# Moving the projection of the second layer's keys from the weighing pass of the first attention into its key pass

## The reference, cut to what matters

```
# layer 0: 8 heads of 64; context normed, keys rotated by position
kv_x = layer_norm(ctx) @ Wkv;  k = rope_rotate_k(k_x);  sim = q k^T;  out = softmax(sim) v
# layer 1: 16 heads of 16; context as it is
k = ctx @ wk + bk;  v = ctx @ wv + bv;  out = softmax(q k^T / 4 + mask) v
```

## Time and profile before

| | us |
|---|---|
| median of 3 runs | 2969.78 (2967.99 to 2975.21) |
| the profiled execution, its time | 2967.38 |
| its span, first to last instruction | 2965.6 |
| key pass, from its first matmul to the first transfer of the weighing pass | about 143.8 to 432.5 |
| weighing pass, to the first transfer behind it | about 432.5 to 945.5 |
| mean granted TensorE clock, share of 2.4 GHz | 0.898 |

### The profile page before, as it was taken

The page is one execution under the profiler, slowest core; times in us unless marked ns, Lnnn a source line. Parts: engine busy times, 40 slices in busy tenths (PEclk is TensorE's granted clock), DMA queues, the critical chain, the costliest instruction groups (busy, mean ns, idle before and its releaser), DMA issues. The chain is left out here.

```text
span 2965.6 us, 58913 instructions
## 1 busy us (share of the span) xinstructions
PE 2399.3 (81%) x22114; PEld 1483.9 (50%) x22114; DVE 1865.8 (63%) x3029; ACT 1212.3 (41%) x1871; POOL 479.5 (16%) x260
## 2 busy tenths in 40 slices
PE   3488869999997393999995779999995336999978
PEld 3333325555554381666663635555554323555547
DVE  7577766666766615666653248778884838777721
ACT  2145533333332324777773223233330133555542
POOL 0055530000000000000000005666551200000000
PEclk7599989999998795999997799999997567999989
DMA  7455553555541164766660523222221144676626
GB/s 238 165 179 193 194 178 101 145 145 151 153 137 57 53 227 123 164 157 158 168 135 24 191 92 115 87 87 87 87 105 34 38 105 96 150 164 149 155 59 228
DMA packets 240402, 390.69 MB, mean 132 GB/s; under 512 B 31281, under 2 KB 201622, under 8 KB 240122
## 3 DMA queue, kind: packets, MB, share of 16 engines
q1 hardware_dynamic: 240250, 388.47, 45.6%
HBM read 310.41 MB, written 78.01 MB: 131 GB/s over the span
## 5 line engine op out<-in xcount | busy, mean ns | idle before, releaser
L2271 PE MATMUL l2x_kf<-l2x_w,l2x_nin 128*128 128x512 f32 x784 | 341.6, 596 | 6.8 <-DMA l2x_nin<-scratch_nT 6.7
L1465 DVE CUSTOM_DVE_ANT_0 l1x_junk<-l1x_pm,l1x_mrow,l1x_top 128x896 bf16<-128x896 f32 x224 | 247.1, 1148 | 107.5 <-PE l1x_pm L1604 105.0
L1465 DVE CUSTOM_DVE_ANT_0 l3x_junk<-l3x_pm,l3x_mrow,l3x_top 128x896 bf16<-128x896 f32 x224 | 246.1, 1148 | 87.1 <-PE l3x_pm L1604 86.6
L1533 ACT ACTIVATE l1x_prob<-l1x_ring,l1x_mask_col 128x512 f32<-128x512 f32 x392 | 247.8, 684 | 114.0 <-PE l1x_ring L1624 112.9
L1536 ACT ACTIVATE l3x_prob<-l3x_ring 128x512 f32<-128x512 f32 x392 | 213.0, 595 | 160.5 <-PE l3x_ring L1628 160.4
L1251 POOL TENSOR_TENSOR l2x_side_rest<-l2x_side_xin,l2x_side_kp 128x1792 f32<-128x1792 f32 x14 | 50.3, 3593 | 1341.4 <-ACT l2x_side_kp L1227 1341.4
L2271 PEld LDWEIGHTS l2x_kf<-l2x_w,l2x_nin 128*128 128x128 f32 x784 | 148.5, 191 | 191.5 <-issue 189.0
L2253 ACT ACTIVATE l2x_fsq<-l2x_f 128x1024 f32<-128x1024 f32 x98 | 103.6, 1057 | 287.4 <-DVE l2x_f L2218 287.4
L2317 POOL TENSOR_TENSOR l2x_gk<-l2x_f,l2x_ks 128x1024 f32<-128x1024 f32 x98 | 182.3, 1896 | 159.9 <-DVEq L2243 159.9
L1055 PE MATMUL l0x_att_pv<-l0x_wv,l0x_att_vin 128*128 128x512 f32 x392 | 194.5, 618 | 1.3 <-DVE l0x_att_tops L936 1.3
L948 DVE TENSOR_TENSOR l0x_att_pt<-l0x_att_ps,l0x_att_tops 128x1024 f32<-128x1024 f32 x99 | 120.9, 1221 | 97.3 <-PE l0x_att_ps L1072 97.2
(11 more groups left out here) (689 smaller groups left out, 4718.8 us busy)
## 6 DMA issues: line engine op xcount, KB each, us to landing
l1x_kt<-scratch_KS SPq DMA_DIRECT2D x84, 448.0 KB, 9.1
l3x_kt<-scratch_KS SPq DMA_DIRECT2D x84, 448.0 KB, 9.1
scratch_KT<-l0x_max_kf SPq DMA_DIRECT2D x28, 896.0 KB, 3.9
l0x_att_kt<-scratch_KT SPq DMA_DIRECT2D x56, 448.0 KB, 7.5
scratch_KS<-l0x_side_kp SPq DMA_DIRECT2D x14, 1344.0 KB, 13.7
scratch_KS<-l2x_side_kp SPq DMA_DIRECT2D x14, 1344.0 KB, 6.0
l0f_w<-L_ffn_exp_w SPq DMA_DIRECT2D x16, 1024.0 KB, 7.0
l1f_w<-L_ffn_W SPq DMA_DIRECT2D x16, 1024.0 KB, 6.5
```

The costliest lines, as they stand in the source:

```text
L1465: dve.tensor_tensor_reduce(junk[x % 2][:, :, :], pm[x % 2][:, :, 0:SPLIT], mrow[b][:, :].rearrange("p (s k) -> p s k", s=2), 1.0, top[1 - ...
L1533: ins = act.activation(into, scores, ACT.Exp, bias=R.mask_col[:, bass.ds(m * TILES + n // 4, 1)])
L2271: last = pe.matmul(pf[u][:, n, :], nin[b][:, c, t * P:(t + 1) * P], w[:, c, n * BANK:(n + 1) * BANK], start=(c == 0), stop=(c == DC - 1))
```

## The change

Four edits go together.

1. **The projection moves.** The key pass also loads the raw context of its chunk (`raw`, one more transfer), PE makes two more projections for it (`other_keys`, tile `p1`, printed as `l0x_max_p`), ACT adds the bias into `k1` (printed as `l0x_max_k`), and SP spills `k1` to a new float32 tensor `scratch_K1`. In the weighing pass `side.project` and `side.evacuate` are gone; `side_xin` is loaded from `scratch_K1` instead of the raw context and split as before.
2. **PSUM.** `pb` had two banks and now has one; `p1` gets the other.
3. **The order.** ACT's order in the key pass becomes that of PE (copy, other keys, rounding, for each half), and the fold of the second half is done one step later, ahead of everything else on DVE. The signal with which PE lets SP load the next chunk (`projected`) moves behind the last `other_keys`.
4. **Two buffers for the parts.** In layer 0 `side_kp` gets two buffers, so that the high part of a chunk waits for the spill two chunks before. Layer 2's side work keeps one.

```diff
@@ rotated_keys, SP
+                    sp.dma_start(raw[b][:, :, :], raw_src[n].squeeze(0)).then_inc(sem(f"raw{b}"), 16)
...
                     sp.dma_start(kt_dram[n].squeeze(0), kf[b][:, :, :]).then_inc(sem(f"spilled{b}"), 16)
+                    after(sp, sem("k1_read"), DC * (number(b, i) + 1))
+                    sp.sem_inc(S.sem("max_begun"), 1)
+                    sp.dma_start(k1_dram[n].squeeze(0), k1[b][:, :, :]).then_inc(sem(f"k1_spilled{b}"), 16)
@@ rotated_keys, DVE
                 def both(ahead, now):
+                    fold_second_of_before(*now)
                     rotate(*ahead, 0)
-                    fold(*now, 0)
+                    fold_first(*now)
                     rotate(*ahead, 1)
-                    fold(*now, 1)
@@ rotated_keys, ACT
+                def other_keys(b, i, c):
+                    if c == 0:
+                        after(act, sem(f"k1_spilled{b}"), i * 16)
+                    after(act, sem("k1_proj"), DC * number(b, i) + c + 1)
+                    act.activation(k1[b][:, c, :], p1[:, 0:MAX_CHUNK], ACT.Identity,
+                                   bias=bias1[:, c:c + 1]).then_inc(sem("k1_read"), 1)
...
                 def both(ahead, now):
                     copy_scores(*now, 0)
+                    other_keys(*ahead, 0)
+                    round_keys(*ahead, 0)
                     copy_scores(*now, 1)
-                    round_keys(*ahead, 0)
+                    other_keys(*ahead, 1)
                     round_keys(*ahead, 1)
@@ rotated_keys, PE
-                    after(pe, sem("b_read"), 2 * number(b, i) if p == 0 else n - 1)
-                    project(pb[p], w_k, b, slice((2 + p) * P, (3 + p) * P), xin).then_inc(sem("b_proj"), 1)
+                    after(pe, sem("b_read"), n)
+                    project(pb, w_k, b, slice((2 + p) * P, (3 + p) * P), xin).then_inc(sem("b_proj"), 1)
...
+                def other_keys(b, i, c):
+                    if c == 0:
+                        after(pe, sem(f"raw{b}"), (i + 1) * 16)
+                    after(pe, sem("k1_read"), DC * number(b, i) + c)
+                    project(p1, w1, b, slice(c * P, (c + 1) * P), raw).then_inc(sem("k1_proj"), 1)
+                    if c == DC - 1:
+                        after(pe, sem("k1_proj"), DC * number(b, i) + DC)
+                        after(pe, sem("a_proj"), 2 * number(b, i) + 2)
                         pe.sem_inc(sem(f"projected{b}"), 1)
...
                 def both(ahead, now):
                     block_of_keys(*ahead, 0)
                     scores(*now, 0)
+                    other_keys(*ahead, 0)
                     block_of_keys(*ahead, 1)
                     scores(*now, 1)
+                    other_keys(*ahead, 1)
@@ attend, PE
-                        if t % TILES < 4:
-                            side.project(pe, 2 * i + t // TILES, t % TILES)
@@ SplitKeys
+        self.kp = [sb(f"kp{b}", [P, 3, DC, CHUNK], BF16) for b in range(self.per_chunk)]
```

More of the change, by code:

```diff
@@ L495, in _, with rotated_keys @@
                 start_counts(pool, S)
-def rotated_keys(nc, S, A, R, qb, w_k, bias_k, top, chunks, seed):
+def rotated_keys(nc, S, A, R, qb, w_k, bias_k, other, top, chunks, seed):
     nc = S.nc
@@ L517, in rotated_keys @@
         xin = [sb(f"xin{b}", [P, DC, MAX_CHUNK]) for b in range(2)]
+        raw = [sb(f"raw{b}", [P, DC, MAX_CHUNK]) for b in range(2)]
         cs = [sb(f"cs{b}", [P, 2, MAX_CHUNK]) for b in range(2)]
@@ L520, in rotated_keys @@
         kf = [sb(f"kf{b}", [P, 4, MAX_CHUNK]) for b in range(2)]
+        k1 = [sb(f"k1{b}", [P, DC, MAX_CHUNK]) for b in range(2)]
         kb = [sb(f"kb{b}", [P, 4, MAX_CHUNK], BF16) for b in range(2)]
@@ L524, in rotated_keys @@
         pa = [ps(f"pa{p}") for p in range(2)]
-        pb = [ps(f"pb{p}") for p in range(2)]
+        pb, p1 = ps("pb"), ps("p1")
         psc = ps("ps", HEADS)
@@ L575, in _ @@
                 dve.wait_ge(S.sem("max_started"), 3)
+                dve.memset(near[1][:, :, :], -3.0e38).then_inc(S.sem("near_begun"), 1)
+                dve.wait_ge(S.sem("near_begun"), 1)
                 for p in range(2):
@@ L914, in _ @@
                         chunks.load(sp, b, i + 1)
-                        side.spill(sp, 2 * i + b)
+                        side.spill(sp, i, b)
                 for b in range(2):
@@ L1188, in load, with spill @@
     def load(self, sp, m):
[L1189 to L1192 removed]
+        after(sp, self.sem("rest"), self.per_chunk * m)
         sp.sem_inc(self.S.sem("side_begun"), 1)
         sp.dma_start(self.xin[:, :, :], self.src[bass.ds(m, 1)].squeeze(0)).then_inc(self.sem("xin"), 16)
[L1196 removed]
+    def spill(self, sp, i, b):
+        m = 2 * i + b
         after(sp, self.sem("low"), self.per_chunk * (m + 1))
@@ L1198, in spill @@
         sp.sem_inc(self.S.sem("side_begun"), 1)
-        sp.dma_start(self.dst[bass.ds(m, 1)].squeeze(0), self.kp[:, :, :, :].rearrange(
-            "p s c k -> p (s c) k")).then_inc(self.sem("spilled"), 16)
-    def project(self, pe, m, n):
-        c, side = n // 2, n % 2
-        if n == 0:
-            after(pe, self.sem("xin"), (m + 1) * 16)
-        after(pe, self.sem("read"), 4 * m + n)
-        for d in range(DC):
-            last = pe.matmul(self.px[:, 0:SPLIT], self.w[:, d, c * P:(c + 1) * P],
-                             self.xin[:, d, side * SPLIT:(side + 1) * SPLIT], start=(d == 0), stop=(d == DC - 1))
-        last.then_inc(self.sem("projected"), 1)
@@ L1212, in evacuate @@
-    def evacuate(self, act, m, n):
-        c, side = n // 2, n % 2
-        if n == 0:
-            after(act, self.sem("rest"), 2 * m)
-        after(act, self.sem("projected"), 4 * m + n + 1)
-        act.activation(self.kf[:, c, side * SPLIT:(side + 1) * SPLIT], self.px[:, 0:SPLIT], ACT.Identity,
-                       bias=self.bias[:, c:c + 1]).then_inc(self.sem("read"), 1)
-    def high(self, act, m, c):
+        sp.dma_start(self.dst[bass.ds(m, 1)].squeeze(0), self.parts(b).rearrange(
+            "p s c k -> p (s c) k")).then_inc(self.sem(f"spilled{b}"), 16)
@@ L1221, in high, with parts @@
+    def parts(self, b):
+        return self.kp[b % len(self.kp)]
+    def high(self, act, i, b, c):
+        m = 2 * i + b
         if c == 0:
-            after(act, self.sem("spilled"), m * 16)
-        if self.proj:
-            after(act, self.sem("read"), 4 * m + 2 * c + 2)
-        elif c == 0:
+            if len(self.kp) == 2:
+                after(act, self.sem(f"spilled{b}"), i * 16)
+            else:
+                after(act, self.sem(f"spilled{1 - b}"), (i + b) * 16)
             after(act, self.sem("xin"), (m + 1) * 16)
-        act.activation(self.kp[:, 0, c, :], self.kf[:, c, :], ACT.Copy).then_inc(self.sem("high"), 1)
@@ L1255, in subtract, with finish @@
             self.sem("low"), 1)
-    def finish(self, sp, m):
-        after(sp, self.sem("spilled"), m * 16)
+    def finish(self, sp, n):
+        for b in range(2):
+            after(sp, self.sem(f"spilled{b}"), n * 16)
 class Heads16:
```

121 lines of the change are left out of this document (62 added, 59 removed).

## The result

The changed kernel takes 2917.74 us (median of 4, 2915.77 to 2918.13), the kernel before in the same session 2972.49 (2967.99 to 2975.3): ratio 0.9815 [0.9801, 0.9829], 1.9% faster. The forecast was 2908, range 2895 to 2930. The profiled execution took 2918.13, its span is 2916.3. In a second session the changed kernel had a ratio of 0.9787 [0.9773, 0.9801]. The two differ by 0.3%, more than either interval allows, so 8 us between kernels of different sessions say nothing.

A forecast was written before the change was run, and what follows sets the result against it. TensorE bounds the weighing pass; in the key pass no engine is full and TensorE waits for VectorE's rotation. 2967.4 - 95.2 + 33 = 2905.2, and the median lies 2.4 above the profiled execution: 2908 us, range 2895 to 2930.

The forecast's parts named there:

- Weighing pass: -95.2 forecast: Weighing pass, TensorE: 56 projections at 1.70 us each taken out, all of it coming back, -95.2 us.
- The rival that it would (+21): Weighing pass: VectorE late in every chunk becomes a new bound, +21 us, 2929; chance 0.12.
- worth 0 in the sum, and it guards the 95.2: Weighing pass: two buffers remove ScalarE's wait for the spill, which would have grown with shorter tiles; 0 in the sum.
- Key pass: +33 forecast: Key pass: 302.0 us against 267.8 with two projections more per chunk, +34.2, with tail and late load together +33.
- 7.91 + 3.04 = **10.95 us a chunk: Key pass: TensorE's own 7.91 us a chunk plus 3.04 for two projections, if TensorE never waits.
- the lower bound of 10.7: Key pass: lowest chunk time, with added projections at 1.49 us each and neighbours less 0.11; upper bound 11.3.
- The tail, -1.9: Key pass end: the last half's scores, copies and fold no longer queue behind one late rounding, about -1.9 us.
- No waits for VectorE, full clock: Key pass: no waits of `pb` for `terms`, TensorE busy nearly throughout, clock 1.00 where it was 0.95.
- the clock still falls: Key pass rival: TensorE's handoffs to VectorE stay; seven half-clock pairs 12 us, 2920, one every chunk 49, 2957; chance 0.10.
- The ring: Key pass: GpSimd join, ScalarE rounding and copies, VectorE fold and rotation, still 9.34 us, 1.6 inside TensorE's 10.95.
- Transfers, hidden at 0: Key pass: 2688 KB a chunk instead of 1792, 251 GB/s in 10.95 us, hidden behind TensorE at no cost.
- The rival of 14.2 us a chunk: Key pass: transfers limited to 194 GB/s set the period, 14.2 us a chunk, +26 in all, 2996; chance 0.04.

The follow-up runs named there:

- the first experiment: Changed kernel, key pass only: SP waits on the last `other_keys` matmul's semaphore itself, TensorE no longer waits there; 2897.08 us, ratio 0.9743 to the kernel before.
- the repeat: The changed kernel unaltered, run again in the second session as base for its experiments; 2911.53 us, ratio 0.9787 to the kernel before.

## Why the forecast was right, and what it missed

- **Weighing pass: -95.2 forecast, -94.3 measured.** 56 projections at 1.70 us came back whole. Tiles 0 and 3 go at the 4.03 us that tiles 4 to 6 had before; VectorE did not become the bound. The rival that it would (+21) fell.
- **Two buffers for the parts, "worth 0 in the sum, and it guards the 95.2".** The sum was right. The size of what it guards was not stated, and it is 66 us of the median (2977.31 - 2911.53), all that the change gains in that session (64.4). The prediction named the wait and not how near it was to TensorE: in the kernel before the exponential stood right behind it.
- **Key pass: +33 forecast, +41.9 measured.** The median missed 2908 by 9.7 us. Between the two profiled executions 62.2 us were forecast and 49.3 measured, 12.9 too many, and 8.9 of these are this term (0.9 are the weighing pass, 3.1 the rest). The step that was mis-sized is "7.91 + 3.04 = **10.95 us a chunk**"; measured 11.25. The 7.91 holds TensorE's wait for its own last matmul at its old price, a block of 3.57 instead of 3.21, 0.36 a chunk. At its new place, in front of the next chunk's block, it idles 0.40 or about 0.79 in turns, the step takes 0.56 or 0.95 longer and the first projection behind it 0.09 more: 0.85 a chunk, 0.49 over the old price. The other way went 0.19: without the wait the sum says 10.95 - 0.36 = 10.59, and the first experiment's chunk takes 10.40 (from scores to the next projection 0.49 each time, where the sum took 0.64 once). That is also why 10.40 lies below the lower bound of 10.7, which still held the wait. Over 26 chunks the 0.30 make 8 us. The late `xin` cost 1.6 over the wait that it replaced, instead of 1, and the first chunk took 12.55 (143.78 to 156.33) instead of 10.95 - 1.0 + 1.9 = 11.85.
- **The tail, -1.9.** From the last half chunk's block to the weighing pass: 22.84 before (411.61 to 434.45), 20.77 after, -2.07.
- **No waits for VectorE, full clock.** Both held. TensorE has no wait for `terms` in the pass, and the granted clock in the steady part is 1.00. The rival "the clock still falls", and with it the Trainium skill's rule ("TensorE: Matmul & The Clock Gate", section "A second HAM failure mode: psum-queue depth-cycling"), has nothing for it here: with `pb` in one bank and a pause of 0.40 to 0.83 us in each chunk the clock stayed up. In the experiments it fell behind some longer waits: 3.56 us at 396.27 without the wait for the last matmul, 3.45 at 603.39 and 1.93 at 415.50 with one buffer, 2.43 at 267.19 with the old order. It stayed up behind 2.04 at 416.62 in the changed kernel, 3.04 at 637.07 with one buffer and most of the 2.43 with the old order. So the length of a wait alone doesn't decide it, and the full clock behind the changed kernel's one late load was in part luck.
- **The ring.** It would have 9.34 us and stand inside 10.95. It does, even inside 10.40. That holds only with ScalarE's new order: with the old one the move costs more than it gives.
- **Transfers, hidden at 0.** 243 GB/s at a share of 0.74, 265 at 0.80 in the first experiment, and taking a sixth of the bytes away leaves the chunks as they are and changes the time by less than can be told. The rival of 14.2 us a chunk fell. Only the late `xin` hangs on the new load, 1.6 us.
- **`xin`.** The one late load is the one foreseen, behind the weighing pass's first chunk. It was dearer in the faster pass: 2.04 us at 11.25 a chunk (1.74 in the repeat), 3.56 and 3.73 at 10.40, there with half-clock projections behind it.
- **Open.** The stages behind both passes took 3.1 us longer in the profiled execution, and scatter by 13 us over all; no run looked for the cause. Part of the 9.7 us may be this and no term of the sum.

## What to carry to other kernels

A signal that an engine sends after waiting for its own last instruction was a pause of its pipeline here. Let the engine that needs the signal wait on that instruction's semaphore itself, above all where the sender bounds the pass. When a bound engine's period gets shorter, look again at every wait that was hidden before: where the next instruction in an in-order queue follows a released one with no gap, little cover may be left. When work is moved into a pass with gaps, see that the order on the engines that empty its buffers follows the producer's; here the move lost more than it gained without that.

## What the runs showed of the hardware

The wait for its own last matmul cost TensorE 0.30 to 0.38 us idle in one place and 0.40 or 0.78 to 0.83, in turns from chunk to chunk, in another; 0.57 and 0.52 were seen at single places. Why the two chunks of an iteration differ wasn't tried. Behind it the first group also took 1.76 us instead of 1.67. The granted clock did not follow the length of a wait: with the old order TensorE went on at half clock in four chunks of the key pass and at full clock in most others, behind the same waits of 2.35 and 2.43 us. A spill of 1344 KB behind the loads of the next chunk had landed only after 13.9 us, while the transfer engines were busy for 0.51 of that pass.
